# Softmax numerators turned without their scale, and a scale on the attention's output that comes by way of the memory

## The chip, the cores and the metric

One Trainium2 chip, one core. The metric is the device time of one launch in microseconds. The kernel is one hand-scheduled program: each engine (TensorE or PE, VectorE or DVE, ScalarE or ACT, GpSimd or POOL, and SP, which issues DMAs) has its own written list of steps, and semaphores order them.

## The reference

Two layers on x (4 batches of 256 tokens, width 256), each with an attention over a context (4 x 256 x 128) and a feed-forward part. What the change touches is the second layer's attention, 16 query heads in 8 pairs, each pair with one key/value head:

```python
q = (text_hidden @ Wq).reshape(B, T_text, N_HEADS, HEAD_DIM).transpose(0, 2, 1, 3)
k = (vision_tokens @ Wk)...; v = (vision_tokens @ Wv)...      # 8 heads, repeated for 16
scores = jnp.einsum('bhtd,bhsd->bhts', q, k) / scale
scores = jnp.where(mask, scores, -jnp.inf)
attn = jax.nn.softmax(scores, axis=-1)
out = jnp.einsum('bhts,bhsd->bhtd', attn, v)
return out.reshape(B, T_text, N_HEADS * HEAD_DIM) @ Wo
```

Ahead of it stand the first layer (attention without heads, then an 8-bit feed-forward part with ternary weights) and a layer norm, behind it the last feed-forward part (8-bit float weights, three products).

## The kernel before, in words

The second attention runs over n = 0 to 31: batch n // 8, pair of heads n % 8, both heads of the pair at once. For each n, in order:

- `queries(n)` (PE), then `q_hi` (ACT) and `q_lo` (DVE): each operand of a product is split in a high and a low part, and each product is three matmuls.
- `scores(n, h)` (PE) for head h; `masked(n, h)` (DVE) adds the mask, takes the row minimum and writes `sm`, which has two buffers (n % 2), each of four tiles k = 0 to 3 (head and token tile) of 128 tokens x 256 keys.
- `exps(n, h)` (ACT): the exponentials, in place, with their row sums in `ssum`.
- `inverse(n)` (DVE, L1569): the reciprocals `srec` of the four sums. `normalise(n)`: ACT multiplies tiles 0 and 1 of `sm` by them (L998), POOL tiles 2 and 3 (L661).
- The probabilities are turned, so that keys lie on the partitions. For n = 0, 1, 2, 30 and 31 PE does it (`probs4`). For the 27 pairs n = 3 to 29, `turn_blocks(n)` (DVE, L1580) turns 32 x 32 blocks of `sm` into the one buffer `blocks`; `blocks_written(n)` (SP, L441) writes it in four DMAs to `block_room` in the memory, and `blocks_read(n)` (L454) reads it back in two halves c as `tp`, rows now in their right places. `turn_blocks(n+1)` waits until all four writes of pair n have landed. `block_room` and `tp` have two rooms each; a read into `tp` waits until `contexts(n-2)` is done.
- `probs(n, c)` (ACT, L992) makes `pT_hi` from `tp`, `probs_low(n, c)` (POOL, L666) makes `tp_lo`.
- `contexts(n, c)` (PE): the attention's output, transposed, in one PSUM bank. `outputs(n)` (ACT, L1004) makes `oT_hi` from the bank, `outputs_low(n)` (DVE, L1594) makes `oT_lo` = bank - `oT_hi`. `attn_out(n, h)` (PE) multiplies by the fused output weights and sums over the batch's heads in bank 6.

The steps of several pairs are interleaved with each other, with the feed-forward tiles of the first layer's other batches (`gate_half`, `value_half`, `ffn_out`), with the rounding of the last part's weights (`eighths`), and near the end with the last part's products (`gate4`, `up4`, `down`). The order of every engine is a written list of calls at the end of its block, and `PASSING` is the written list of which PSUM bank each product uses, in PE's order. Between `scores(n)` and `contexts(n)` PE works on four or five other pairs.

Of the kernel before, what the change touches and what calls it, by code (L numbers as in the profile page):

```python
# [23 lines left out]
def xattn_ffn_kernel(nc, x, ctxT, mask, wq0T, bq, wk0T, bk, w_norm, wgvT, woutT, wq, wk, wv, wo,  # L24
# [29 lines left out]
    with ExitStack() as ctx:  # L54
# [63 lines left out]
        with ExitStack() as ffn:  # L118
            wgv8 = tile(ffn, "wgv8", [P, KD, 2 * HID], BF16)
            wout8 = tile(ffn, "wout8", [P, KH, D], BF16)  # L120
            wn = tile(ffn, "wn", [P, D])
            gbuf = tile(ffn, "gbuf", [P, 2, TB, D])
# [21 lines left out]
            wscale = tile(ffn, "wscale", [P, 2])  # L144
        with ExitStack() as last:
# [6 lines left out]
        tile(ctx, "ffn_room", [P, 9368])  # L152
# [27 lines left out]
        oT_hi = tile(ctx, "oT_hi", [P, 2, 2 * TOK], F32R)  # L180
        oT_lo = tile(ctx, "oT_lo", [P, 2, 2 * TOK], F32R)
# [7 lines left out]
        block_room = nc.dram_tensor("block_room", [2 * S, 2 * TOK], F32).ap()  # L189

# [3 lines left out]
        def bank16(n):  # L194
# [32 lines left out]
        pT_lo_pool, norm_act = sem("pT_lo_pool"), sem("norm_act")  # L227
# [26 lines left out]
        PASSING = [("project", 0, 4), ("context", 0, 2), ("xn", 0, 3), ("energy", 0, 4), ("project", 1, 5), ("xn", 1, 6),  # L254
                   ("probs", 0, 7), ("energy", 1, 0), ("mean", 0, 4), ("mix", 0, 2), ("project", 2, 7), ("project", 3, 0),
                   ("kv", 0, 2), ("probs", 1, 7), ("energy", 2, 6), ("mix", 1, 7), ("energy", 3, 5), ("kv", 1, 1), ("xn", 2, 0),
                   ("kv", 2, 7), ("kv", 3, 0), ("hidden_in", 0, 4), ("mean", 1, 3), ("probs", 2, 2), ("mix", 2, 4),
                   ("gate", 0, 5), ("gate", 1, 2), ("gate", 2, 7), ("value", 0, 1), ("value", 1, 3), ("value", 2, 5),
                   ("vo", 0, 0), ("probs", 3, 7), ("gate", 3, 3), ("xn", 3, 0), ("value", 3, 2), ("turn", 0, 3), ("vo", 1, 7),
                   ("gate", 4, 6), ("turn", 1, 1), ("vo", 2, 0), ("value", 4, 4), ("turn", 2, 5), ("qk", 0, 6), ("qk", 1, 3),  # L260
                   ("gate", 5, 1), ("vo", 3, 2), ("gate", 6, 4), ("hidden", 0, 1), ("hidden", 1, 0), ("out", 0, 5),
                   ("out", 1, 0), ("turn", 3, 4), ("value", 5, 7), ("vo", 4, 2), ("gate", 7, 5), ("mix", 3, 1), ("turn", 4, 5),
# [7 lines left out]
                   ("gate", 10, 0), ("s", 13, 7), ("q", 7, 1), ("gate", 11, 3), ("rows", 1, 2), ("ctx", 3, 0), ("s", 14, 3),  # L270
                   ("s", 15, 4), ("q", 8, 5), ("q", 9, 2), ("q", 10, 4), ("s", 16, 7), ("s", 17, 1), ("ctx", 4, 7),
                   ("s", 18, 1), ("s", 19, 2), ("value", 9, 1), ("ctx", 5, 5), ("value", 10, 2), ("value", 11, 0), ("s", 20, 3),
# [3 lines left out]
                   ("s", 29, 7), ("out", 4, 0), ("out", 5, 2), ("ctx", 10, 3), ("value", 12, 0), ("rows", 2, 5), ("s", 30, 4),  # L276
# [96 lines left out]
        def as_f32(ap):  # L373
            return ap.bitcast(F32)
# [5 lines left out]
        def _(sp):  # L380
# [51 lines left out]

            def blocks_written(n):
                k = turns_before(n)
                sp.wait_ge(blocks_done, k + 1)
                if k >= 2:
                    sp.wait_ge(blocks_in[0], 16 * (k - 1))
                    sp.wait_ge(blocks_in[1], 16 * (k - 1))
# [2309 lines left out]
```

## Time and profile before

| | |
|---|---|
| median of 3 runs | 319.15 us (318.28 to 320.42) |
| profiled execution | 319.45 us, its span 317.4 us |
| mean granted TensorE clock | 0.993 |
| busy, share of the span | PE 93%, PEld 82%, ACT 81%, DVE 79%, POOL 69% |
| DMA | 44.59 MB in 54609 packets, mean 140 GB/s |

The span runs from the first to the last instruction of the profiled execution; the run's time has 2.05 us beside it. PEld is the loading of weights, beside PE's matmuls. Matmuls are pipelined, so a busy PE need not be at its peak: a 128x256 matmul lasts 283 ns in the rows, and in a dense stretch one begins each 120 ns.

### The profile page before, as it was taken

The page shows a single profiled execution, that of the slowest core. Times are in us where ns is not written, and L with a number is a line of the kernel's source. Part 1 is how long each engine was busy: PE and PEld are TensorE (multiplying, and loading weights), DVE is VectorE, ACT ScalarE, POOL GpSimd, SP SyncE. Part 2 cuts the span into 40 slices and gives each one's busy share as a digit, 9 for nine tenths or more (in the row PEclk, how much of TensorE's full clock was granted, in tenths as well). Part 3 has the DMA queues.
Part 4 walks back from the last instruction along what each step waited for, and adds up shares of the span by engine and source line. Part 5 has one row for each costly group of instructions (what it writes and reads, how often), then busy time and mean ns, then how long its engine had stood idle before and what let it go on. Part 6 is the DMA issues. An engine that isn't in the chain of part 4 may idle for free.

```text
span 317.4 us, 6401 instructions
## 1 busy us (share of the span) xinstructions
PE 294.9 (93%) x1981; PEld 258.8 (82%) x1992; DVE 252.2 (79%) x713; ACT 258.5 (81%) x607; POOL 217.9 (69%) x290
## 2 busy tenths in 40 slices
PE   3676999999999999999989999999999999999994
PEld 2465566889988987899779989889999998989784
DVE  3789698989888789888889788897877595766674
ACT  0869796489999989999997897788899998975350
POOL 3786663566887788797877897878897696772001
PEclk9999799999999999999999999999999999999999
DMA  7994602002046867678637566687665466200201
GB/s 219 380 350 135 176 0 68 1 1 76 5 81 179 245 168 199 165 209 202 180 88 207 150 179 162 165 221 203 147 188 151 116 197 200 69 2 0 68 1 66
DMA packets 54609, 44.59 MB, mean 140 GB/s; under 512 B 11696, under 2 KB 45104, under 8 KB 54576
## 3 DMA queue, kind: packets, MB, share of 16 engines
q1 hardware_dynamic: 54016, 43.93, 49.1%
q8 instruction: 16, 0.26, 0.4%
q10 hardware_dynamic: 560, 0.26, 0.3%
q14 instruction: 17, 0.14, 0.1%
HBM read 27.01 MB, written 15.20 MB: 133 GB/s over the span
## 4 chain that ended last, share of the span: by engine, by line
PE 21%; ACT 15%; POOL 8%; issue 5%; DVE 1%; ACTq 0%; POOLq 0%; DVEq 0%
PE pb L2015 14%; PE pb L2278 4%; ACT sm L980 4%; POOL tp_lo L666 4%; ACT pT_hi L992 3%; PE pb L2312 2%; POOL xn L588 1%; ACT sm L998 1%; ACT L980 1%; POOL sm L661 1%; ACT L1019 1%; ACT fuse L1019 1%; ACT q_hi L975 1%; ACT oT_hi L1004 1%; POOL rstd L582 1%
## 5 line engine op out<-in xcount | busy, mean ns | idle before, releaser
L666 POOL TENSOR_TENSOR tp_lo<-tp,pT_hi 128x512 fp32r<-128x512 f32 x54 | 69.2, 1297 | 20.9 <-ACT pT_hi L992 20.8
L980 ACT ACTIVATE sm<-sm,smin 128x256 f32<-128x256 f32 x128 | 63.6, 503 | 1.1 <-DVE smin L1563 0.7
L1563 DVE CUSTOM_DVE_ANT_0 sm<-pb,mask_all 128x256 f32<-128x256 f32 x128 | 47.5, 419 | 4.0 <-PE pb L2015 3.6
L1580 DVE STREAM_TRANSPOSE blocks<-sm 128x1024 f32<-128x1024 f32 x27 | 33.5, 1240 | 7.0 <-DMA block_room<-blocks 6.1
L2015 PE MATMUL pb<-ctx_hi,q_hi 128*128 128x256 f32 x128 | 37.8, 295 | 0.5 <-DVE q_lo L1550 0.4
L2015 PE MATMUL pb<-xT_hi,m_hi 128*128 128x256 f32 x128 | 37.2, 291 | 0.1
L2015 PE MATMUL pb<-n_hi,oT_hi 128*128 128x256 f32 x128 | 37.1, 290 | 0.1
L2015 PE MATMUL pb<-xT_hi,m_lo 128*128 128x256 f32 x128 | 36.2, 283 | 0.0
L2015 PE MATMUL pb<-xT_lo,m_hi 128*128 128x256 f32 x128 | 36.2, 283 | 0.0
L2015 PE MATMUL pb<-ctx_hi,q_lo 128*128 128x256 f32 x128 | 36.2, 282 | 0.0
L2015 PE MATMUL pb<-ctx_lo,q_hi 128*128 128x256 f32 x128 | 36.1, 282 | 0.0
L2015 PE MATMUL pb<-n_lo,oT_hi 128*128 128x256 f32 x128 | 36.1, 282 | 0.0
L2015 PE MATMUL pb<-n_hi,oT_lo 128*128 128x256 f32 x128 | 36.1, 282 | 0.0
L661 POOL TENSOR_SCALAR sm<-sm,srec 128x256 f32<-128x256 f32 x64 | 30.4, 488 | 8.3 <-DVE srec L1569 8.2
L992 ACT ACTIVATE pT_hi<-tp 128x512 fp32r<-128x512 f32 x54 | 32.2, 623 | 3.4 <-PE pb L2015 3.2
L2015 PE MATMUL pb<-pT_hi,cr_hi 128*128 128x512 f32 x64 | 27.1, 424 | 2.3 <-POOL tp_lo L666 1.6
L998 ACT ACTIVATE sm<-sm,srec 128x256 f32<-128x256 f32 x64 | 28.6, 504 | 0.7 <-DVE srec L1569 0.7
L582 POOL TENSOR_TENSOR rstd<-ve,nhalf 128x2 f32<-128x2 f32 (+1 forms) x16 | 13.3, 834 | 20.1 <-DVE ve L1412 17.4
L1594 DVE TENSOR_TENSOR oT_lo<-pb,oT_hi 128x512 fp32r<-128x512 f32 x32 | 21.7, 681 | 6.0 <-ACT oT_hi L1004 5.9
L2015 PEld LDWEIGHTS pb<-ctx_hi,q_hi 128*128 128x128 f32 x128 | 24.4, 190 | 2.4 <-DVE q_lo L1550 0.9
L2015 PEld LDWEIGHTS pb<-n_hi,oT_hi 128*128 128x128 f32 x128 | 24.4, 191 | 1.4 <-DVE oT_lo L1594 0.5
L975 ACT ACTIVATE q_hi<-pb 128x512 fp32r<-128x512 f32 x32 | 18.8, 588 | 8.0 <-PE pb L2015 7.9
(195 smaller groups left out, 946.4 us busy)
## 6 DMA issues: line engine op xcount, KB each, us to landing
block_room<-blocks SPq DMA_DIRECT2D x108, 128.0 KB, 2.5
tp<-block_room SPq DMA_DIRECT2D x54, 256.0 KB, 3.1
w_raw<-in_w SPq DMA_DIRECT2D x4, 576.0 KB, 4.2
wraw<-in_wgvT SPq DMA_DIRECT2D x4, 512.0 KB, 7.4
wraw<-in_woutT SPq DMA_DIRECT2D x2, 512.0 KB, 10.6
out<-xb SPq DMA_DIRECT2D x4, 256.0 KB, 2.2
xa<-in_x SPq DMA_DIRECT2D x3, 256.0 KB, 4.6
xb<-in_ctxT SPq DMA_DIRECT2D x2, 256.0 KB, 6.1
```

What stands on the lines that cost most here:

```text
L582: g.tensor_tensor(rstd[:, planes, tiles(b)], ve[:, planes, tiles(b)], nhalf[:, planes, tiles(b)], ALU.pow).then_inc(rstd_done, 1)
L661: g.tensor_scalar(sm[:, n % 2, k, :], sm[:, n % 2, k, :], srec[:, n % 2, k:k + 1], 1.0, ALU.mult, ALU.mult).then_inc(norm_done, 1)
L666: g.tensor_tensor(tp_lo[:, z, c, :], tp[:, z, c, :], as_f32(pT_hi[:, c, :]), ALU.subtract).then_inc(pT_lo_pool, 1)
L975: a.activation(q_hi[:], bank(passing_bank("q", n)), ACT.Copy, scale=-SCALE).then_inc(q_hi_done, 1)
L980: a.activation(sm[:, n % 2, k, :], sm[:, n % 2, k, :], ACT.Exp, bias=smin[:, n % 2, k:k + 1], scale=-1.0, accum_out=ssum[:, n % 2, k:k + 1 ...
L992: a.activation(pT_hi[:, c, :], whole, ACT.Copy).then_inc(pT_hi_done, 1)
L998: a.activation(sm[:, n % 2, k, :], sm[:, n % 2, k, :], ACT.Identity, scale=srec[:, n % 2, k:k + 1]).then_inc(norm_act, 1)
L1563: v.tensor_tensor_reduce(out=sm[:, n % 2, k, :], in0=bank(passing_bank("s", 2 * n + h))[:, (k % 2) * S:(k % 2 + 1) * S], in1=mask_all[:, b ...
L1580: v.transpose(blocks[:].rearrange("p g k b -> p k g b"), sm[:, n % 2, :, :].rearrange("p k (g b) -> p k g b", b=32)).then_inc(blocks_done, 1)
L1594: v.tensor_tensor(oT_lo[:, n % 2, :], bank(passing_bank("ctx", n)), as_f32(oT_hi[:, n % 2, :]), ALU.subtract).then_inc(oT_lo_done, 1)
L2015: last = t_.matmul(dst, a_, b_, start=start and k == 0, stop=stop and k == n - 1, skip_group_check=check)
L2278: last = t_.matmul(dst, weight[:, k, i * P:(i + 1) * P], part[:, k, tok], start=n == 0, stop=n == 2 * KD - 1)
```

## The change

For the pairs turned by blocks (n = 3 to 29) the exponentials aren't multiplied by `srec`. They are turned, written, read back and used by `contexts` as they are. The reciprocals take a way of their own: `inverse(n)` writes them 32 times side by side (`sr`, 128 x 4 x 32), a second transpose in `turn_blocks(n)` turns them (`sr_turned`, 128x128), a fifth DMA in `blocks_written(n)` writes four partitions of it (pieces of 32 floats) to `factor_room`, and `factors_read(n)` reads the row of 512 factors back onto all 128 partitions as `rb` (two buffers). It counts on the same semaphore as the second half of `tp`. `outputs_scaled(n)` on VectorE multiplies the bank by `rb` into `o_raw`, from which ScalarE makes `oT_hi` and GpSimd `oT_lo`. ScalarE's `normalise` is gone; for the five other pairs GpSimd scales all four tiles. `down` waits for its own piece of the last weights in place of all. All five engines' lists and `PASSING` are written anew, with the same steps otherwise.

```diff
@@ SP @@
 def blocks_written(n):
     k = turns_before(n)
-    sp.wait_ge(blocks_done, k + 1)
+    sp.wait_ge(blocks_done, 2 * (k + 1))
...
     for i in range(4):
         sp.dma_start(rows[:, :, i * P:(i + 1) * P], blocks[32 * i:32 * (i + 1), :, :, :].rearrange("a g k b -> a g (k b)")).then_inc(blocks_out, 16)
+    sp.dma_start(factor_room[k % 2, :].rearrange("(k i b) -> i k b", k=2 * TB, b=32),
+                 sr_turned[0:P:32, :].rearrange("i (k b) -> i k b", b=32)).then_inc(blocks_out, 16)

+def factors_read(n):
+    k = turns_before(n)
+    if k >= 2:
+        sp.wait_ge(o_scaled, k - 1)
+    sp.wait_ge(blocks_out, 80 * (k + 1))
+    if k >= 1:
+        sp.wait_ge(blocks_in[1], 32 * k)
+    sp.dma_start(rb[:, k % 2, :], factor_room[k % 2:k % 2 + 1, :].broadcast_to([P, 2 * TOK])).then_inc(blocks_in[1], 16)
@@ GpSimd @@
 def normalise(n):
     pool.wait_ge(srec_done, n + 1)
-    for k in (2, 3):
+    for k in range(4):
...
+def outputs_low(n):
+    if n == FIRST_TURNED:
+        pool.wait_ge(oT_lo_done, n)
+    pool.wait_ge(oT_hi_done, n + 1)
+    g.tensor_tensor(oT_lo[:, n % 2, :], o_raw[:, n % 2, :], as_f32(oT_hi[:, n % 2, :]), ALU.subtract).then_inc(oT_lo_done, 1)
@@ ScalarE @@
 def probs(n, c):
     if by_blocks(n):
-        act.wait_ge(blocks_in[c], 16 * (turns_before(n) + 1))
+        act.wait_ge(blocks_in[c], (16, 32)[c] * (turns_before(n) + 1))
...
-def normalise(n):
-    act.wait_ge(srec_done, n + 1)
-    for k in (0, 1):
-        a.activation(sm[:, n % 2, k, :], sm[:, n % 2, k, :], ACT.Identity, scale=srec[:, n % 2, k:k + 1]).then_inc(norm_act, 1)

 def outputs(n):
-    act.wait_ge(oT_ps, n + 1)
+    if by_blocks(n):
+        act.wait_ge(o_scaled, turns_before(n) + 1)
+        whole = o_raw[:, n % 2, :]
+    else:
+        act.wait_ge(oT_ps, n + 1)
+        whole = bank(passing_bank("ctx", n))
     if n >= 2:
         act.wait_ge(attn_ps, n - 1)
-    a.activation(oT_hi[:, n % 2, :], bank(passing_bank("ctx", n)), ACT.Copy).then_inc(oT_hi_done, 1)
+    a.activation(oT_hi[:, n % 2, :], whole, ACT.Copy).then_inc(oT_hi_done, 1)
@@ VectorE @@
 def inverse(n):
     dve.wait_ge(exp_done, 4 * (n + 1))
-    v.reciprocal(srec[:, n % 2, :], ssum[:, n % 2, :]).then_inc(srec_done, 1)
+    if by_blocks(n):
...
+        v.reciprocal(sr[:, n % 2, :, :], ssum[:, n % 2, :].rearrange("p (k a) -> p k a", a=1).broadcast_to([P, 4, 32])).then_inc(srec_done, 1)
+    else:
+        v.reciprocal(srec[:, n % 2, :], ssum[:, n % 2, :]).then_inc(srec_done, 1)

 def turn_blocks(n):
     k = turns_before(n)
-    dve.wait_ge(norm_act, 2 * (n + 1))
-    dve.wait_ge(norm_done, 2 * (n + 1))
+    dve.wait_ge(srec_done, n + 1)
     if k >= 1:
-        dve.wait_ge(blocks_out, 64 * k)
+        dve.wait_ge(blocks_out, 80 * k)
...
     v.transpose(blocks[:].rearrange("p g k b -> p k g b"), sm[:, n % 2, :, :].rearrange("p k (g b) -> p k g b", b=32)).then_inc(blocks_done, 1)
+    v.transpose(sr_turned[:], sr[:, n % 2, :, :].rearrange("p k b -> p (k b)")).then_inc(blocks_done, 1)

+def outputs_scaled(n):
+    dve.wait_ge(oT_ps, n + 1)
+    dve.wait_ge(blocks_in[1], 32 * (turns_before(n) + 1))
+    dve.wait_ge(attn_ps, n - 1)
+    v.tensor_tensor(o_raw[:, n % 2, :], bank(passing_bank("ctx", n)), rb[:, turned_room(n), :], ALU.mult).then_inc(o_scaled, 1)
@@ TensorE @@
 def down(c, n):
...
-    if c == 0 and n == 0:
-        pe.wait_ge(w8_done, B * EIGHTS)
+    if c < KI:
+        pe.wait_ge(w8_done, -(-(2 * KD * INNER + (i + 1) * D) // PIECE))
@@ SP's list, from blocks_written(14) on (one stretch of the new order) @@
 blocks_written(14)
 blocks_read(14)
 blocks_written(15)
+factors_read(14)
 blocks_read(15)
 blocks_written(16)
+factors_read(15)
 blocks_read(16)
 blocks_written(17)
+factors_read(16)
@@ the end of GpSimd's list @@
+outputs_low(28)
 normalise(31)
+outputs_low(29)
+eighths(15)
+eighths_out(15)
 rows4(2)
-eighths(15)
-eighths_out(15)
 rows4(3)
@@ VectorE's list before added3(3); stats4(2) stood ahead of outputs_low(26) @@
+outputs_low(30)
 outputs_low(31)
+stats4(2)
+fuse_low(3)
 added3(3)
 stats4(3)
```

## Rows read from the trace of the kernel before

**Rows 1.** The page, busy times: us, share of the span, instructions of each engine.

```profile
PE 294.9 (93%) x1981; PEld 258.8 (82%) x1992; DVE 252.2 (79%) x713; ACT 258.5 (81%) x607; POOL 217.9 (69%) x290
```

**Rows 2.** Windows of the span: busy us of each engine, clock, DMA share, GB/s.

```profile
0.00:20.00 20.00, 11.44 (x50) 9.27 (x51) 12.29 (x42) 10.08 (x24) 11.91 (x25) 1.00 0.90 303
20.00:40.00 20.00, 15.70 (x80) 10.93 (x80) 16.28 (x51) 16.47 (x31) 14.46 (x21) 0.91 0.62 197
40.00:60.00 20.00, 19.04 (x122) 13.37 (x122) 18.45 (x46) 14.56 (x23) 11.84 (x14) 1.00 0.09 27
60.00:100.00 40.00, 39.38 (x297) 35.54 (x299) 35.08 (x116) 36.34 (x93) 25.59 (x39) 1.00 0.20 49
100.00:160.00 60.00, 58.53 (x418) 52.85 (x422) 50.34 (x148) 58.67 (x140) 49.18 (x62) 1.00 0.72 196
160.00:220.00 60.00, 58.18 (x418) 53.06 (x419) 51.03 (x155) 49.52 (x137) 49.37 (x63) 1.00 0.65 171
220.00:280.00 60.00, 59.84 (x401) 54.45 (x400) 44.83 (x123) 56.54 (x136) 46.37 (x57) 1.00 0.55 150
280.00:300.00 20.00, 19.41 (x131) 17.40 (x131) 13.77 (x24) 10.84 (x19) 7.95 (x12) 1.00 0.04 14
```

**Rows 3.** What PE waited for, 60 to 317.4 us: us in total, times, longest.

```profile
PE pb L2015 <- POOL tp_lo L666: 1.6, 3, 1.1
```

**Rows 4.** Groups of instructions by line: busy us, mean ns, then idle time before.

```profile
L666 POOL TENSOR_TENSOR tp_lo<-tp,pT_hi 128x512 fp32r<-128x512 f32 x54 | 69.2, 1297 | 20.9 <-ACT pT_hi L992 20.8
...
L1580 DVE STREAM_TRANSPOSE blocks<-sm 128x1024 f32<-128x1024 f32 x27 | 33.5, 1240 | 7.0 <-DMA block_room<-blocks 6.1 <-ACT sm L998 0.5
...
L661 POOL TENSOR_SCALAR sm<-sm,srec 128x256 f32<-128x256 f32 x64 | 30.4, 488 | 8.3 <-DVE srec L1569 8.2
L998 ACT ACTIVATE sm<-sm,srec 128x256 f32<-128x256 f32 x64 | 28.6, 504 | 0.7 <-DVE srec L1569 0.7
...
L1594 DVE TENSOR_TENSOR oT_lo<-pb,oT_hi 128x512 fp32r<-128x512 f32 x32 | 21.7, 681 | 6.0 <-ACT oT_hi L1004 5.9
...
L1569 DVE RECIPROCAL srec<-ssum 128x4 f32<-128x4 f32 x32 | 5.4, 170 | 9.4 <-ACT sm L980 9.1
...
L1426 DVE RECIPROCAL erec<-esum 128x2 f32<-128x2 f32 x4 | 0.6, 159 | 0.1
```

**Rows 5.** VectorE's timeline, the first, two adjoining and the last block transpose: start, us.

```profile
93.95 1.25 DVE L1580 STREAM_TRANSPOSE blocks<-sm 128x1024 f32<-128x1024 f32 x1
...
219.41 1.25 DVE L1580 STREAM_TRANSPOSE blocks<-sm 128x1024 f32<-128x1024 f32 x1 [0.85 <-DMA block_room<-blocks]
...
225.09 1.25 DVE L1580 STREAM_TRANSPOSE blocks<-sm 128x1024 f32<-128x1024 f32 x1 [1.14 <-DMA block_room<-blocks]
...
265.32 1.25 DVE L1580 STREAM_TRANSPOSE blocks<-sm 128x1024 f32<-128x1024 f32 x1
```

**Rows 6.** DMA issues: size, median us to landing; then `blocks`' writes, minimum to maximum.

```profile
block_room<-blocks SPq DMA_DIRECT2D x108, 128.0 KB, 2.5
tp<-block_room SPq DMA_DIRECT2D x54, 256.0 KB, 3.1
...
dsc<-in_down_scale SPq DMA_DIRECT2D x1, 128.0 KB, 3.8
...
gsc<-in_gate_scale SPq DMA_DIRECT2D x1, 3.0 KB, 3.6
...
DMA to landing us min/median/max: 2.0/2.5/4.2
```

**Rows 7.** SP's queue, two stretches (219 to 226, 232 to 234 us): start, us.

```profile
219.36 0.82 SPq L454 DMA_DIRECT2D tp<-block_room  x2
220.68 2.38 SPq L441 DMA_DIRECT2D block_room<-blocks  x4
...
232.46 1.84 SPq L441 DMA_DIRECT2D block_room<-blocks  x4
```

**Rows 8.** Waits of the whole span: us in total, times, longest.

```profile
DVE blocks L1580 <- DMA block_room<-blocks: 6.1, 10, 1.1
```

More of the change, by code:

```diff
@@ L1168, in _ @@
+            outputs(5)
+            exps(9, 1)
+            queries(11)
+            probs(7, 0)
+            probs(7, 1)
             exps(10, 0)
-            probs(7, 0)
-            outputs(5)
-            normalise(9)
+            probs(8, 0)
+            outputs(6)
             exps(10, 1)
-            probs(7, 1)
-            queries(11)
-            normalise(10)
             rounded(4)
-            outputs(6)
-            probs(8, 0)
+            probs(8, 1)
             outputs(7)
-            probs(8, 1)
@@ L1752, in _ @@
             outputs_low(1)
-            turn_blocks(3)
+            m_low(7)
             masked(5, 0)
             masked(5, 1)
+            q_low(6)
+            turn_blocks(4)
             second(2)
+            second(3)
+            third_stats(1)
+            outputs_low(2)
+            masked(6, 0)
             inverse(5)
-            q_low(6)
-            second(3)
-            turn_blocks(4)
-            third_stats(1)
-            masked(6, 0)
-            outputs_low(2)
-            masked(6, 1)
@@ L1765, in _ @@
-            q_low(7)
-            turn_blocks(5)
-            eighths(2)
-            gated_half(4, 0)
-            third_low(1)
-            inverse(6)
+            turn_blocks(5)
+            masked(6, 1)
+            eighths(2)
+            outputs_scaled(3)
+            inverse(6)
+            third_low(1)
+            gated_half(4, 0)
+            q_low(7)
+            turn_blocks(6)
             masked(7, 0)
+            q_low(8)
             masked(7, 1)
-            turn_blocks(6)
-            q_low(8)
+            masked(8, 0)
@@ L1775, in _ @@
             inverse(7)
-            outputs_low(3)
-            masked(8, 0)
+            q_low(9)
+            gated_half(4, 1)
+            outputs_scaled(4)
+            turn_blocks(7)
             masked(8, 1)
-            q_low(9)
-            turn_blocks(7)
-            inverse(8)
-            masked(9, 0)
-            outputs_low(4)
-            masked(9, 1)
-            q_low(10)
-            gated_half(4, 1)
-            eighths(3)
+            q_low(10)
+            masked(9, 0)
+            masked(9, 1)
@@ L1788, in _ @@
+            eighths(3)
+            outputs_scaled(5)
+            inverse(8)
+            turn_blocks(8)
             u_max(4)
+            u_scales(4)
+            gated_half(5, 0)
+            masked(10, 0)
             inverse(9)
-            turn_blocks(8)
-            masked(10, 0)
-            gated_half(5, 0)
-            u_scales(4)
+            turn_blocks(9)
             masked(10, 1)
-            outputs_low(5)
-            turn_blocks(9)
-            inverse(10)
+            outputs_scaled(6)
@@ L1798, in _ @@
             gated_half(5, 1)
+            eighths(4)
             q_low(11)
             u_max(5)
-            eighths(4)
-            outputs_low(6)
+            outputs_scaled(7)
+            masked(11, 0)
+            q_low(12)
             u_scales(5)
-            masked(11, 0)
+            inverse(10)
+            turn_blocks(10)
+            outputs_scaled(8)
             masked(11, 1)
-            q_low(12)
-            turn_blocks(10)
+            masked(12, 0)
+            masked(12, 1)
@@ L1808, in _ @@
             inverse(11)
-            outputs_low(7)
-            masked(12, 0)
             q_low(13)
-            masked(12, 1)
-            outputs_low(8)
             turn_blocks(11)
-            inverse(12)
-            added3(0)
-            masked(13, 0)
-            masked(13, 1)
-            eighths(5)
-            q_low(14)
+            masked(13, 0)
+            added3(0)
+            eighths(5)
+            outputs_scaled(9)
+            masked(13, 1)
+            q_low(14)
+            second(4)
@@ L1821, in _ @@
+            inverse(12)
             inverse(13)
             turn_blocks(12)
+            second(5)
             masked(14, 0)
-            outputs_low(9)
-            second(4)
             masked(14, 1)
-            second(5)
             third_stats(2)
+            outputs_scaled(10)
+            turn_blocks(13)
+            q_low(15)
+            eighths(6)
             gated_half(6, 0)
-            q_low(15)
-            turn_blocks(13)
-            outputs_low(10)
-            eighths(6)
@@ L1834, in _ @@
             third_low(2)
+            masked(15, 0)
             inverse(14)
-            masked(15, 0)
+            outputs_scaled(11)
+            gated_half(6, 1)
             masked(15, 1)
-            outputs_low(11)
+            u_max(6)
+            q_low(16)
+            inverse(15)
             turn_blocks(14)
-            gated_half(6, 1)
-            inverse(15)
-            q_low(16)
+            masked(16, 0)
             stats4(0)
             eighths(7)
-            masked(16, 0)
+            outputs_scaled(12)
@@ L1891, in _ @@
             third_stats(3)
-            outputs_low(17)
+            outputs_scaled(17)
             masked(22, 0)
@@ L1932, in _ @@
             eighths(13)
-            outputs_low(22)
+            inverse(26)
             turn_blocks(26)
-            fused(0)
+            outputs_scaled(23)
+            q_low(29)
             masked(28, 0)
@@ L1938, in _ @@
             masked(28, 1)
-            outputs_low(23)
-            q_low(29)
-            inverse(28)
             eighths(14)
@@ L2661, in _ @@
             contexts(31, 1)
+            down(2, 1)
             attn_out(30, 0)
```

971 lines of the change are left out of this document (486 added, 485 removed), and 51 rows, old and new, of the table PASSING.

## The prediction

> **What bounds the kernel now.** I read the busy times first [rows 1]: TensorE 93%, the other four engines' busy shares between 69% and 82%. A busy share is an average, so the windows come next [rows 2]. From 60 to 280 us TensorE is idle for 0.62, 1.47, 1.82 and 0.16 us of its windows (window minus PE busy), and for 0.59 us from 280 to 300: 4.7 us in 240 us. Before 60 us it is idle for 8.6 + 4.3 + 1.0 = 13.8 us, and of the 22.5 us that it idles in all (317.4 less 294.9) the last 4.0 lie behind 300 us, where the last output is scaled, added and stored. In the window from 20 to 40 us the granted clock is 0.91, so part of it ran at the lower level (1.2 of 2.4 GHz) after a stretch with much idle time; no other window to 300 us shows that. The third view is what PE waited for from 60 us on [rows 3]: GpSimd's `tp_lo` 1.6 us in three waits; every other line waited less. So this is a TensorE-bound kernel with two soft spots: the start, and about 5 us of small waits. The change doesn't alter the number or the shape of the matmuls, so beyond these two it can give nothing.
>
> Of the other engines ScalarE is the nearest to a bound: 58.7 of 60 us from 100 to 160, 56.5 of 60 from 220 to 280 [rows 2]. Yet PE waits on it for next to nothing, so relieving it is worth at most what PE idles.
>
> **The change part by part** (27 of the 32 pairs of heads are turned by blocks).
>
> ScalarE loses all its `normalise` work: 64 instructions, 28.6 us busy [rows 4], 0.45 us each. Nothing else is added there; `outputs` reads SBUF for PSUM at the same shape. Per turned pair 0.9 us goes. A pair takes 6.59 us (171.4 us from the first to the last block transpose over 26 steps [rows 5]), so 60 us hold 9.1 pairs and the window of 58.7 us falls to 50.5.
>
> GpSimd loses two scalings of a turned pair, 0.95 us (L661, 30.4 us over 64 [rows 4]), and gains `outputs_low`. Its nearest row is L666, the same subtraction of 128x512 in SBUF: 1.30 us. Net +0.35 us a pair, and 0.95 us more for each of the five unturned pairs: 9.4 + 4.8 = 14 us, hidden as GpSimd goes from 49.4 to 52.6 of 60 us [rows 2].
>
> VectorE swaps `outputs_low` (0.68 us, PSUM and SBUF, L1594) for `outputs_scaled`, a multiplication of the same shape and sources: zero. The reciprocal grows from 4 to 128 columns, and there is a second block transpose, of 128x128. The trace has neither. The big transpose takes 1240 ns for 1024 columns [rows 4]; with a fixed part like the reciprocal's 170 ns that is 1.04 ns a column, so 0.30 us for 128 columns (lower end: an eighth, 0.16). For the reciprocal, 2 columns took 159 ns and 4 took 170. The lower end is no growth, the upper is that slope, 5.5 ns a column, +0.68 us. I take +0.13 us, the pace of the transpose, because four columns can't carry a slope of a few ns. So +0.43 us a pair, 51.0 to 54.9 of 60 us from 160 to 220: hidden.
>
> The latency of a pair changes on both sides. Ahead of the transpose 0.9 us goes. Behind `contexts` the chain was ScalarE 0.6, VectorE 0.7; now it is VectorE 0.7, ScalarE 0.6, GpSimd 1.3: 1.3 us more. The written order gives PE other work between `contexts(n, 1)` and `attn_out(n, 0)`, for turned pairs never less than 36 matmuls, as between `contexts(4, 1)` and `attn_out(4, 0)`. At one matmul in 0.144 us (60 us over 418 [rows 2]) these are 5.2 us against a chain of 2.6 us. I cost it at nothing; without that cover it would be up to 1.3 us a pair. The new wait in `outputs_scaled` is on the landed factors; behind it in VectorE's queue stand `masked` and `q_low`, for which PE waits. But `probs(n, 1)` on ScalarE already waits for the same count before PE can do `contexts`, so it is never late there. It is late, if at all, at `probs(n, 1)`: a broadcast of 128 rows took 3.8 us to land against 3.1 us for a half of `tp` [rows 6], plus 0.4 us of issue, so 1.1 us more; for 11 pairs `factors_read(n)` stands behind `blocks_written(n+1)`, with five issues of 0.46 us ahead: some 3 us. A half of `tp` can be read once `contexts(n-2)` is done, that is two steps (13.2 us) less one contexts (1.4 us) ahead; 3.5 us to land, 1.2 and 2.6 us on ScalarE and GpSimd leave 4.5 us. It holds on average, and not where two contexts come close. GpSimd already waits 20.8 us for `pT_hi` [rows 4], so this cover is thin: I put 0.5 us on it.
>
> SP's queue gets two more issues a pair: the factors' write (0.46 us) and read (0.4 us). It had 1.8 to 2.4 us of issue for the four writes (1.84 us are 0.46 for one) and 0.8 for the reads, in 6.59 us [rows 7], so it has room. But `blocks` is one buffer, and `turn_blocks(n+1)` waits until all of pair n's writes have landed. That loop is the tightest thing in the trace: 219.41 to 225.09 us is 5.68 us [rows 5], VectorE stood still for 1.14 us of it, and in 10 of 27 cases it waited so [rows 8]. With the change it gains 0.25 us (the small transpose, less overlap) and the fifth issue, 0.46 us, whose landing may come sooner than a block's (2.0 us at the least, 2.5 in the median) or later (a small load took 3.6 us [rows 6]). That is +0.0 to +1.6 us, and the loop comes to 5.9 to 7.5 us. I take +0.4 and 6.3, near the blocks' own rows, since it is a write to the same memory in the same queue. PE's own pace is 6.59 less its idle time there (3.4 us over 26), 6.46 us. So it holds the pace by a hair, and costs nothing in sum; uneven steps cost perhaps 0.5 us.
>
> The Trainium skill speaks against this write (DMA: Bandwidth & Descriptors, section Specifications): below 512 bytes a transfer is done as read-modify-write. The pieces here are 128 bytes, and no row of before has a write of that size. By the blocks' rows the loop costs nothing, by the rule it would be rival (b).
>
> The broadcast adds 256 KB to a pair's 1 MB: the DMA share from 100 to 160 us of 0.72 [rows 2] becomes 0.9 at the most. Landings of the writes queued behind it may come later; that is in the loop's upper end.
>
> The two ends and the orders: all five hand-written orders and the banks are laid out anew. The start depends on loads and on the first batch's chain, which the change doesn't touch; `gate_value(0)` is loaded one transfer earlier, two transposes move. I count zero, with 4 us either way as the bounds (a third of the 13.8 idle us). At the end `normalise(31)` takes four scalings on GpSimd, 1.9 us instead of 0.93 beside ScalarE's 0.9, ahead of `outputs_low(29)`, and `stats4(2)` moves in front of `added3(3)`: +0.5 us. Splitting the wait for `w8` lets one `down` go earlier, worth nothing where PE is busy.
>
> Sum: of 4.7 us of idle time after 60 us I give back half, since ScalarE was 98% busy in 100 to 160 and its lateness is behind part of `tp_lo`'s: -2.4. Then +0.5 probs, +0.5 loop, +0.5 end: -0.9. From the profiled 319.45 us (span 317.4, 2 us around it) that is 318.5; the median of the runs is 0.3 lower, so **318.2 us**.
>
> **The rivals.**
> (a) *All waits go.* ScalarE's relief and the new order return the whole 4.7 us and 2 to 4 us of the start: 319.15 - 7 = 312. For it: ScalarE is the fullest engine beside PE and gives up 8 us of 60. Against: PE hardly waited for it.
> (b) *The block buffer becomes the bound.* Once the loop exceeds 6.46 us, each further tenth costs 26 x 0.1 = 2.6 us. With a late landing of the factors, loop 6.8 us: +8.8 less the waits it replaces (3.4), 324.5; at 7.5 us, 343. For it: the loop's 10 waits, the fifth write, the fuller DMA. Against: the buffer ran at 5.5 to 5.7 us, and 6.3 is below the pace.
> (c) *The wide reciprocal is slow.* At the upper slope VectorE gets +0.98 us a pair, 8.9 us per window of 60: 59.9 of 60. With no slack its waits for others' results in the turned stretch can't be absorbed; half of the 12 us or so that it has there: +6, 325. It decides above 0.8 us for 128 columns. The skill has a rule for this (VectorE: DVE Perf Modes, First, the fixed hardware budget): a reciprocal is an iterated divide with a repeat count of 8. With VectorE at 0.96 GHz (Trainium Kernel Development and Optimization, NeuronCore Architecture) that is an estimate of 8.3 ns a column, a microsecond more for 128, and this rival would be the forecast. The 11 ns that two columns more took are below its 17, which speaks rather against it.
> (d) *Nothing moves:* PE is the bound and the waits only change their place, 319. This is within the forecast's own case.
>
> **How the numbers follow.** One per cent, 3.2 us, is about what can be told from no change here. The forecast with (d): 0.50, of which 0.06 falls below 316 and 0.04 above 322.3. (a) 0.24. (b) 0.19, (c) 0.07. So faster 0.30, within 1% 0.40, slower 0.30. The likeliest case's own range is 315 to 322; to hold 8 in 10 I go to 311.5, which takes in (a), and to 326, which takes in (c) and (b) up to a loop of 6.9 us.
>
> **What would show it.** PE idle time from 60 to 300 us below 4.7 us, the busy times of ScalarE near 230 us, GpSimd 232, VectorE 264. `sr` near 0.30 us. Block transposes 6.3 us apart where they wait for the landing, and 26 steps in 168 to 172 us; more than 175 is (b). `pT_hi` of the second half waiting for the factors' broadcast would show in PE's waits for `tp_lo`. The prediction is wrong if the start moves by more than 4 us, if the write of 128-byte pieces lands after 3 us or more, or if the reciprocal takes over 0.8 us.

## The result and the profile after

The changed kernel takes 346.04 us (median of 3 runs, 346.03 to 347.15) against 319.15: the ratio is 1.0831, 95% interval 1.0754 to 1.0908. The forecast was 318.2 and its range ended at 326, so it was wrong by 27 us. The profiled run is 346.04 us with a span of 344.2. Where single executions of an experiment fell into a slower state of the chip, its time below is the median of the others, while some expectations name the median of all.

The page of the kernel after, busy times, to be read against [rows 1]:

```profile
PE 302.6 (88%) x1981; PEld 259.3 (75%) x1992; DVE 276.5 (80%) x740; ACT 238.2 (69%) x543; POOL 232.6 (68%) x273
```

No engine is full. PE's 1981 matmuls are the same ones, in 27 us more of span. The windows of the kernel after, against [rows 2]:

```profile
60.00:100.00 40.00, 37.41 (x272) 32.73 (x273) 35.20 (x107) 30.45 (x77) 27.33 (x41) 1.00 0.25 64
100.00:160.00 60.00, 55.05 (x374) 47.40 (x376) 51.15 (x138) 45.74 (x113) 41.81 (x42) 0.97 0.70 194
160.00:220.00 60.00, 50.37 (x344) 44.38 (x346) 51.85 (x140) 42.09 (x97) 45.41 (x49) 0.97 0.69 177
220.00:280.00 60.00, 56.38 (x382) 50.50 (x381) 49.89 (x130) 42.77 (x110) 46.75 (x48) 1.00 0.66 188
```

PE idles 2.6, 5.0, 9.6 and 3.6 us here, 20.8 in all, where it idled 4.1. It does 1372 matmuls in these 220 us where it did 1534; at 0.144 us each that is 23 us, so some 6 us more are inside its busy time. The granted clock is 0.97 in two windows, those in which PE stood for 5.0 and 9.6 us, so short parts of them ran at the lower of the two levels. That can be part of the 6 us, but it isn't the cause of the loss: o8 below is 17 us slow at a granted clock of 1.00.

VectorE's timeline, the first, a pair in the middle and the last block transpose, against [rows 5]:

```profile
92.66 1.25 DVE L1608 STREAM_TRANSPOSE blocks<-sm 128x1024 f32<-128x1024 f32 x1 [0.61 <-PE pb L2053]
...
129.55 1.25 DVE L1608 STREAM_TRANSPOSE blocks<-sm 128x1024 f32<-128x1024 f32 x1
...
136.61 1.25 DVE L1608 STREAM_TRANSPOSE blocks<-sm 128x1024 f32<-128x1024 f32 x1 [1.55 <-DMA factor_room<-sr_turned]
...
289.85 1.25 DVE L1608 STREAM_TRANSPOSE blocks<-sm 128x1024 f32<-128x1024 f32 x1 [1.57 <-DMA factor_room<-sr_turned]
```

The first stands 1.3 us earlier than before, the last 24.5 us later: 197.2 us over 26 steps, 7.58 us a step for 6.59. These 25.8 us are practically the whole loss. It is made evenly in the turned stretch; the start is unchanged, and from the last transpose to the end it is 54.4 us for 52.1.

The groups by line in the kernel after, against [rows 4]:

```profile
L723 POOL TENSOR_TENSOR oT_lo<-o_raw,oT_hi 128x512 fp32r<-128x512 f32 x27 | 35.5, 1315 | 9.9 <-ACT oT_hi L1060 9.9
L1608 DVE STREAM_TRANSPOSE blocks<-sm 128x1024 f32<-128x1024 f32 x27 | 33.4, 1238 | 8.5 <-DMA factor_room<-sr_turned 7.6 <-PE pb L2053 0.6
...
L1596 DVE RECIPROCAL sr<-ssum 128x128 f32<-128x128 f32 x27 | 25.6, 947 | 1.1 <-ACT sm L1037 0.9
...
L1616 DVE TENSOR_TENSOR o_raw<-pb,rb 128x512 f32<-128x512 f32 x27 | 18.2, 674 | 5.7 <-PE pb L2053 5.1 <-DMA tp<-block_room 0.6
L1060 ACT ACTIVATE oT_hi<-o_raw 128x512 fp32r<-128x512 f32 x27 | 16.9, 624 | 10.0 <-DVE o_raw L1616 10.0
...
L1609 DVE STREAM_TRANSPOSE sr_turned<-sr 128x128 f32<-128x128 f32 x27 | 7.3, 269 | 0.0
```

The reciprocal took 947 ns for the forecast 300. The others cost what was forecast. But new waits stand beside them: ScalarE 10.0 us for `o_raw`, GpSimd 9.9 us for `oT_hi`, and these in a list of waits of the kernel after (60 to 330 us; us in total, times, longest), against [rows 3, 8]:

```profile
POOL tp_lo L717 <- ACT pT_hi L1049: 23.6, 21, 2.3
...
ACT pT_hi L1049 <- DMA rb<-factor_room: 8.6, 6, 3.5
DVE blocks L1608 <- DMA factor_room<-sr_turned: 7.6, 9, 1.6
ACT pT_hi L1049 <- DMA tp<-block_room: 6.4, 4, 2.7
PE pb L2053 <- POOL tp_lo L717: 6.0, 8, 1.7
...
PE pb L2053 <- POOL oT_lo L723: 3.0, 3, 1.7
```

No line of it is 27 us. Every stage of the pair waits a little for the one before, so this list alone doesn't tell which of them is the cause.

### The profile page after: what moved, and what is told of

It reads as the page before. It is cut to its first block, busy times and chain, and to the rows that moved or that the text cites. A ratio compares the mean times of both kernels' runs of the same rounds, so it can differ in the third digit from the quotient of the medians.

```text
span 344.2 us, 6468 instructions
## 1 busy us (share of the span) xinstructions
PE 302.6 (88%) x1981; PEld 259.3 (75%) x1992; DVE 276.5 (80%) x740; ACT 238.2 (69%) x543; POOL 232.6 (68%) x273
## 4 chain that ended last, share of the span: by engine, by line
PE 40%; ACT 16%; DMA 15%; DVE 11%; issue 6%; SPq 5%; POOL 5%; DVEq 0%; ACTq 0%; POOLq 0%
PE pb L2053 24%; DMA factor_room<-sr_turned 6%; PE pb L2315 4%; SPq L450 4%; ACT sm L1037 4%; DMA rb<-factor_room 2%; DVE sr L1596 2%; PE pb L2350 2%; PE pb L2128 2%; DMA w_raw<-in_w 2%; ACT pT_hi L1049 2%; DMA tp<-block_room 2%; DVE q_lo L1574 2%; POOL tp_lo L717 2%; ACT q_hi L1032 1%
## 5 line engine op out<-in xcount | busy, mean ns | idle before, releaser
L1049 ACT ACTIVATE pT_hi<-tp 128x512 fp32r<-128x512 f32 x54 | 33.3, 626 | 29.1 <-PE pb L2053 14.0
L723 POOL TENSOR_TENSOR oT_lo<-o_raw,oT_hi 128x512 fp32r<-128x512 f32 x27 | 35.5, 1315 | 9.9 <-ACT oT_hi L1060 9.9
L2053 PE MATMUL pb<-pT_hi,cr_hi 128*128 128x512 f32 x64 | 27.9, 436 | 9.0 <-POOL tp_lo L717 6.0
L2053 PEld LDWEIGHTS pb<-xT_hi,m_hi 128*128 128x128 f32 x128 | 24.8, 194 | 5.2 <-DVE xT_lo L1563 3.2
L1574 DVE SCALAR_TENSOR_TENSOR q_lo<-pb,q_hi 128x512 fp32r<-128x512 f32 x32 | 21.6, 675 | 8.8 <-ACT q_hi L1032 8.8
```

The source lines that it names most:

```text
L723: g.tensor_tensor(oT_lo[:, n % 2, :], o_raw[:, n % 2, :], as_f32(oT_hi[:, n % 2, :]), ALU.subtract).then_inc(oT_lo_done, 1)
L1049: a.activation(pT_hi[:, c, :], whole, ACT.Copy).then_inc(pT_hi_done, 1)
L1574: v.scalar_tensor_tensor(q_lo[:], bank(passing_bank("q", n)), -SCALE, as_f32(q_hi[:]), ALU.mult, ALU.subtract).then_inc(q_lo_done, 1)
L2053: last = t_.matmul(dst, a_, b_, start=start and k == 0, stop=stop and k == n - 1, skip_group_check=check)
```

## The experiments

The kernel before, run beside them, took 319.1 to 319.6 us. The first four expectations name their theories in words. After them: L, several costs of nearly equal weight that cover one another; O, the changed kernel's own written orders; C, the longer chain from a context to its outputs; N, the removal of the normalising.

**One cost of the changed kernel at a time.** e1: the reciprocal on 4 columns again (`sr` cleared once, 4 of 128 columns written):

```diff
-v.reciprocal(sr[:, n % 2, :, :], ssum[:, n % 2, :]...broadcast_to([P, 4, 32]))
+v.reciprocal(sr[:, n % 2, :, 0], ssum[:, n % 2, :])
```

> The changed kernel (346.04 us) with the reciprocal on 4 columns (one per tile) in place of 128: only one column of each 32 is used after the transpose, so the result is the same. Theory R, the wide reciprocal (947 ns against 170, 27 times, 21 us of VectorE) is the main cause: 325 us or less. Theory L, the landing of the fifth write in the one-buffer loop is the main cause: VectorE's freed time turns into waiting for the landing, 339 to 343 us. Theory O, the new order of the lists is the cause: 340 to 346 us.

345.2 us, ratio 1.0799 (1.0777 to 1.0822). VectorE's busy time fell from 276.5 to 260.6 us, and its wait for the factors' write rose from 7.6 to 14.0 us. Much of the freed time became waiting.

e2: the factors' transpose and write ahead of the blocks':

```diff
+v.transpose(sr_turned[:], ...)
 v.transpose(blocks[:]..., sm...)
-v.transpose(sr_turned[:], ...)
```

> The changed kernel with the factors' transpose and their write put ahead of the blocks' transpose and writes, so that the fifth write's issue and landing lie beside the big transpose. Nothing is left out. The loop from one block transpose to the next, now some 7.0 us where it waits, would be 6.0 to 6.3. Theory L: 26 steps of 0.7 us and more come back, 325 to 330 us. Theory R: 342 to 346 us, and the waits for the landing vanish from VectorE's rows. Theory W, that the second half of the probabilities waits for the factors' read: no change beyond 2 us.

346.59 us, 1.0838 (1.0766 to 1.0911). It gives nothing back.

e3: no traffic of the factors (the outputs are multiplied by ones, so the division is left out):

```diff
-sp.dma_start(factor_room[...], sr_turned[0:P:32, :]...)
-factors_read(n)                       # all 27
+v.memset(rb[:], 1.0)                  # once
```

> The changed kernel without the factors' write and read; the outputs are multiplied by ones, so the attention's outputs of the 27 pairs are not divided by their sums. The wide reciprocal, both transposes, the multiplication and all orders stay. It removes at once the fifth issue, its landing, the read's issue, its traffic and the wait for it at the second half of the probabilities. Theory L or W: 322 to 328 us. Theory R: 338 to 344 us. Theory O: 340 or more.

339.02 us, 1.0624 (1.0595 to 1.0653): 7 us come back, 20 stay.

e4: a semaphore of its own for the read, so that `probs(n, 1)` doesn't wait for it:

```diff
-sp.dma_start(rb[...], ...).then_inc(blocks_in[1], 16)
+sp.dma_start(rb[...], ...).then_inc(factors_in, 16)
```

> The changed kernel with a semaphore of its own for the factors' read, so that the second half of the probabilities waits for its own half alone, and only the multiplication waits for the factors. Theory W (ScalarE waited 8.6 us for that read, the engine behind it 6 us more): 335 to 339 us. Theories R and L: 343 to 346 us.

345.74 us, 1.0825 (1.0773 to 1.0878). It gives nothing back, though ScalarE's 8.6 us of waits for `rb` are gone.

**Costs together, and the orders.** o1: both costs out of the changed kernel (e3 with the edit of e1; no division):

> Third experiment plus the narrow reciprocal: the changed kernel's five written orders, with the factors neither written nor read (the outputs are multiplied by ones, so the division by the sums is left out for the turned pairs) and the reciprocal again on 4 columns. What is left of the change is the ordinary multiplication by ones on DVE, the small transpose, the subtraction moved to GpSimd and the new orders. Theory L (several loops of nearly equal length, each hiding the others, so that one alone taken out gives nothing back): with the two costs of the loop both out the time falls to 318 to 326 us. Theory O (the new written orders are slow by themselves, whatever the costs): it stays at 333 to 339 us, near the 339.0 us with the factors' traffic alone left out.

336.99 us, 1.0547 (1.0491 to 1.0602). Theory L falls as it stood: 17.6 us stay with both costs gone.

e5: the three repairs (e1, e2, e4) in one kernel, nothing left out:

> The changed kernel with all three repairs at once, nothing left out of the computation: the reciprocal on 4 columns, the small transpose and the factors' write ahead of the blocks', and a semaphore of its own for the factors' read. Theory L: the step between block transposes falls from 7.58 to 6.7 to 7.1 us and the time to 326 to 337 us. Theory O: 341 to 346 us, as with each repair alone.

340.99 us, 1.0684 (1.0622 to 1.0745): 5 us come back.

For theory O the changed kernel's work was put into the written orders of before. My first placing put each scaling on VectorE early in that list (one place of it; the subtraction goes to GpSimd):

```diff
 eighths(8)
+outputs_scaled(14)
 turn_blocks(16)
...
-outputs_low(14)
```

> All the work of the changed kernel, the wide reciprocal and the factors' traffic included, but issued in the written orders of the kernel before: the scalings stand on DVE as soon as their contexts can be there, the subtractions on GpSimd before the next probabilities but one, the factors' read right behind the blocks' read. Theory O: 319 to 328 us. Theory L: 340 to 352 us, since every cost is still there.

> The orders of the kernel before (as in the run above) with the reciprocal on 4 columns and a semaphore of its own for the factors' read; the whole computation is there. Theory O: 316 to 322 us, the reciprocal's 25 us on DVE now worth little. Theory L: 326 to 338 us, as much as the same repairs give in the new orders. Were it under 319 us it would beat both kernels.

466.21 us (o2) and 447.36 us (o3, a single execution; its three others took 457 to 824 us, so it has no ratio). They test nothing of theory O. The waits of o2 (60 to 450 us) say what happened:

```profile
DVE o_raw L1616 <- PE pb L2053: 148.5, 26, 10.9
ACT sm L1037 <- DVE smin L1587: 70.7, 21, 9.4
```

VectorE stood 148.5 us at the head of its queue for contexts, with `masked` and `q_low` behind it, for which ScalarE and PE waited. Scalings a few steps too early (that of pair 14 stands eight steps ahead of its place in o5) cost 109 us between o2 and o5, the dependent steps on ScalarE and GpSimd placed anew with them. So the next three took each place from the trace of before: `outputs_scaled(n)` ahead of the first step that began after `contexts(n)` had ended, ScalarE's rounding and GpSimd's subtraction 0.8 and 1.4 us on.

> The whole work of the changed kernel, every cost of it included, issued in the written orders of the kernel before, each new step put at the place in its engine's list at which the trace of the kernel before shows its operands ready: the scaling at the end of the context's last matmul, ScalarE's rounding 0.8 us later, GpSimd's subtraction 0.6 us after that (the runs with the orders of before above put the scaling too early, and DVE stood 148 us waiting for contexts). Theory O (the changed kernel's own written orders are slow): 319 to 330 us. Theory L (the costs in the loop are what is slow, in any order): 340 to 352 us.

> The same orders, with the reciprocal on 4 columns and a semaphore of its own for the factors' read; the whole computation is there. Theory O: 316 to 326 us. Theory L: 328 to 340 us. A third theory, C (the longer chain from a context to its outputs' rounding, over DVE, ScalarE and GpSimd, is what holds it, in any order and with the costs away): within 2 us of 337.

> The same orders, with the reciprocal on 4 columns and no factors' traffic (the outputs are multiplied by ones, so the division by the sums is left out for the turned pairs). Left of the change: ScalarE's normalising gone, the multiplication on DVE, the subtraction on GpSimd. Theory O: 312 to 320 us. Theory C: 330 to 338 us, as the 337.0 us with the same work in the changed kernel's orders. Theory L: 312 to 326 us.

o5 356.89 us (1.1174), o6 352.13 us (1.1017), o8 335.94 us (1.0523, 1.0474 to 1.0573). Theory O falls: without the two costs it is 336 us in these orders and 337 in the new ones. With them the new orders are 11 us better than the old ones as I filled them (346.0 against 356.9).

**The removed part alone.** d1: the turned pairs' `normalise` left out on both engines of the kernel before (no division), nothing added:

```diff
-normalise(n)                          # ScalarE and GpSimd, n = 3 to 29
```

> The kernel before with the removed part alone: the turned pairs' exponentials are not multiplied by their sums' reciprocals, on ScalarE or on GpSimd, and nothing takes the place of it (the division is left out); contexts, rounding and the subtraction on DVE as before. This prices what the change takes away. Theory C (the longer chain from context to outputs is what costs 17 us in both runs without the factors' traffic): 312 to 319 us, so that the chain's steps make the whole difference to 336. Theory N (it is the removal itself that does harm, by moving work together or taking the normalising's slack out of the queues): 328 to 337 us.

316.57 us, 0.9907 (0.9882 to 0.9932). The removal brings 3.0 us; theory N falls. The windows of one stretch, d1 and then o8:

```profile
60.00:300.00 240.00, 236.76 (x1670) 215.13 (x1669) 194.24 (x563) 193.17 (x468) 153.44 (x176) 1.00 0.52 140
```

```profile
60.00:300.00 240.00, 223.13 (x1552) 197.59 (x1560) 195.93 (x572) 184.67 (x447) 185.99 (x204) 1.00 0.53 137
```

VectorE does about the same in both. In o8 PE has 13.6 us less and 118 matmuls fewer.

**The way from the context to the outputs.** d2: o8 with the subtraction on VectorE again (no division):

```diff
-g.tensor_tensor(oT_lo, o_raw, oT_hi, ALU.subtract)     # GpSimd
+v.tensor_tensor(oT_lo, o_raw, oT_hi, ALU.subtract)     # VectorE, behind ScalarE's rounding
```

> The run o8 (orders of before, narrow reciprocal, no factors' traffic, outputs multiplied by ones) with one change: the subtraction of the rounded outputs stands on DVE again (0.68 us from o_raw), where it stood before, in place of GpSimd's 1.30 us. Theory C in the form that it is GpSimd's queue (the subtraction waits there for ScalarE, and the next probabilities' subtraction, 1.3 us twice, stands behind it): 318 to 325 us. Theory C in the form that DVE's scaling ahead of ScalarE's rounding makes the chain too long: 332 to 338 us.

337.59 us, 1.0538 (1.05 to 1.0576). So it isn't GpSimd's queue alone. d4: the scaling out of the chain but not out of the queue. ScalarE and `outputs_low` read PSUM as before; VectorE multiplies as many elements, waiting for the same context, into a tile that nothing reads (no division):

```diff
-act.wait_ge(o_scaled, ...); whole = o_raw[:, n % 2, :]
+act.wait_ge(oT_ps, n + 1); whole = bank(passing_bank("ctx", n))
-v.tensor_tensor(o_raw[...], bank(...), rb[...], ALU.mult)
+v.tensor_tensor(rb[:, 1, :], rb[:, 0, :], rb[:, 0, :], ALU.mult)
```

> The same work on every engine as in d2 (338.2 us), but the scaling is out of the chain: ScalarE rounds the context straight from PSUM as before, DVE subtracts from PSUM as before, and between them DVE makes a multiplication of the same 128x512 elements, which still waits for the context, into a tile that nothing reads (the division is left out). If the length of the chain context, DVE, ScalarE is what costs (DVE's place for the scaling must be late enough for the context and early enough for ScalarE): 318 to 324 us. If it is DVE's load and its wait for the context, whoever waits for it: 332 to 340 us.

323.61 us, 1.0147 (1.0109 to 1.0185). Taking the scaling out of the chain gives back 14.0 us. The edit brings two things with it that weren't tested apart: ScalarE's rounding and VectorE's subtraction stand in their places of the kernel before again (some 30 places in their lists), and the context's bank is freed by the subtraction, not by the scaling. The other 7.0 us over d1 are VectorE's load with its wait, and the smaller parts of the change that d4 keeps. In the profiled runs only 5.1 us of the difference lie between the first and the last block transpose; 2.3 us lie ahead of the first, where no scaling has run yet. What PE waited for (60 to 330 us), first in d4, then in d2:

```profile
PE pb L2016 <- DVE q_lo L1505: 1.7, 4, 0.5
```

```profile
PE pb L2019 <- DVE oT_lo L1571: 7.8, 7, 1.9
...
PE pb L2019 <- DVE q_lo L1509: 3.3, 4, 1.9
PE pb L2019 <- POOL tp_lo L679: 3.0, 3, 1.9
```

and in o8, where GpSimd subtracts:

```profile
PE pb L2020 <- POOL tp_lo L679: 7.7, 15, 1.6
...
PE pb L2020 <- POOL oT_lo L685: 4.0, 4, 2.1
```

With the subtraction on VectorE, PE waits for `oT_lo` itself. With it on GpSimd, it waits for the probabilities' subtraction, which now shares that queue. The length between is in the timelines: from the end of the last matmul of a pair's contexts to the end of its `oT_lo`, mean of the 27 turned pairs, it took 4.4 us in the kernel before, 4.8 in d4, 6.4 in d2 and 6.9 in the kernel after. In o8 it stayed at 4.4, and there PE waits more for the probabilities in the same queue. d2 and d4 aren't equal in VectorE's load either: d2's subtraction took 953 ns and d4's 678, d4's multiplication 823 ns and d2's 681, so VectorE has 5.4 us more in d2. By the price of VectorE's load below that is 1 or 2 of the 14.0 us.

Where the 953 ns come from is in the trace. The subtractions of d2 (both sources in SBUF), then those of d4 (one source in PSUM), minimum, median and maximum in ns:

```profile
L1571 DVE TENSOR_TENSOR oT_lo<-o_raw,oT_hi x27: 650/695/1812, 114.3 to 301.9; 128x512 fp32r<-128x512 f32 x27
```

```profile
L1568 DVE TENSOR_TENSOR oT_lo<-pb,oT_hi x32: 650/683/694, 89.1 to 292.2; 128x512 fp32r<-128x512 f32 x32
```

Of d2's 27, 16 took 650 to 720 ns. The other 11 began while an instruction of GpSimd had 0.29 to 1.26 us left, and each ended 0.54 to 0.55 us after that one. None of d4's 32 did so, though GpSimd worked beside most of them. So an instruction of VectorE with both sources in SBUF waits here for most of GpSimd's running ones (two of d2's 16 began beside an `rstd` and an `xn` and didn't wait), and one with a source in PSUM doesn't.

e6: the same move in the changed kernel with its three repairs, the whole computation there:

> The whole computation of the changed kernel in its own orders with the three repairs of e5 (341.0 us), and the subtraction of the rounded outputs on DVE, behind ScalarE's rounding, in place of GpSimd. DVE goes from 262 to 280 us busy, GpSimd from 232 to 197. Theory C as GpSimd's queue: 324 to 332 us. Theory C as the scaling's place in the chain: 340 to 348 us.

349.37 us, 1.0953 (1.0902 to 1.1004): 8 us worse than e5. Here 21 of the 27 subtractions were held up by GpSimd in that way, and they took 1102 ns in the mean. The subtraction fits neither engine.

**One added cost at a time in the kernel before.** b1: a second reciprocal, 128 columns wide, that nothing reads:

```diff
+v.reciprocal(wide[:], ssum[:, n % 2, :]...broadcast_to([P, 4, 32]))
 v.reciprocal(srec[:, n % 2, :], ssum[:, n % 2, :])
```

> The kernel before with one part of the change alone: for each turned pair DVE makes one more reciprocal, 128 columns wide as in the changed kernel, into a tile that nothing reads. It adds 27 times 0.95 us to DVE, 25.6 us in all, from 252 to 278 us busy. If DVE has room for it (as e1 said of the changed kernel): 319 to 323 us. If DVE's load is itself a loop near the bound, as theory L holds: 325 to 335 us.

324.27 us, 1.0148 (1.0075 to 1.0221): 5 us for 25.4 us of VectorE. That is between its two cases.

The factors' traffic, write and read (b3), and then the write alone (b2):

```diff
 for i in range(4): sp.dma_start(block_room..., blocks...)
+sp.dma_start(factor_room[k % 2, :]..., blocks[0:P:32, 0, :, :]).then_inc(blocks_out, 16)
 for c in range(SC): sp.dma_start(tp..., block_room...)
+sp.dma_start(rb[...], factor_room[...].broadcast_to(...)).then_inc(blocks_in[1], 16)   # b3 only
```

> The kernel before with the factors' traffic alone: a fifth write of 4 partitions in 128-byte pieces behind the four of the blocks, counted with them, and a read of 2 KB into all 128 partitions behind the blocks' read, counted with its second half, on which the second rounding of the probabilities waits; nothing reads what it brings. By e3 against the changed kernel the traffic is worth 7 us: 323 to 329 us. If the traffic costs only in a kernel whose other queues are already late: 319 to 322 us.

> The kernel before with the fifth write alone (4 partitions, 128-byte pieces, counted with the four of the blocks), and no read of the factors. With write and read it took 337.6 us. If the write, which holds the block buffer until it has landed, is the traffic's cost: 332 to 338 us. If it is the read, in SyncE's queue ahead of the next writes and in ScalarE's wait for the probabilities' second half: 319 to 324 us.

With the read it is 335.56 us, 1.0537 (1.0466 to 1.0609), without it 320.26 us, 1.0028 (1.0 to 1.0055). So the write costs 0.6 us and the read about 15. SP's queue in b3:

```profile
183.54 0.82 SPq L461 DMA_DIRECT2D tp<-block_room  x2
184.41 0.43 SPq L464 DMA_DIRECT2D rb<-factor_room  x1
184.95 2.08 SPq L444 DMA_DIRECT2D block_room<-blocks  x4
187.07 0.98 SPq L445 DMA_DIRECT2D factor_room<-blocks  x1
190.38 0.82 SPq L461 DMA_DIRECT2D tp<-block_room  x2
```

VectorE's block transposes began at 183.62 and 190.45; the second waited for the write of 187.07, which by the chain of work took 3.26 us from there to its landing, with the read's 256 KB ahead of it. The waits of b3, VectorE and SP:

```profile
DVE blocks L1590 <- DMA factor_room<-blocks: 21.8, 14, 3.2
```

```profile
SPq L460 <- DMA factor_room<-blocks: 27.0, 13, 2.5
...
SPq L441 <- DMA rb<-factor_room: 20.3, 8, 3.5
...
SPq L461 <- DMA rb<-factor_room: 5.6, 3, 2.9
```

SP now stands 25.9 us for landings of `rb`, at the next pair's writes and at its own reads, and everything behind it in the queue goes later. In the chain of work that ended last, from 95 to 285 us, SP's issues and the landings of its DMAs have 78% and PE's products 5%; in the kernel before these products are the largest part of that chain, with 23%. This is the price of b3's place for the read, right behind the blocks' read; in the kernel after it often stands elsewhere. In the traces the steps between block transposes that ended in a wait for the landing have a median of 6.0 us before (10 steps), 6.55 in b2 (12), 6.93 in b3 (14) and 7.45 in the kernel after (9). PE's pace was 6.46.

## Why the prediction was wrong

The costs as they stack up, each from the run named: 319.6 us before; -3.0 for the removal (d1); +7.0 for VectorE's scaling and small transpose as load (d4); +14.0 for the scaling's place in the chain (d2, with what d4's edit brought along); -1.7 with the subtraction on GpSimd (o8); +21.0 for traffic and wide reciprocal (o5, where b3 and b1 alone gave 16.0 and 5.1); -10.9 for the new orders: 346.0. The sum closes by construction. What speaks for it is that traffic and reciprocal, measured apart in the kernel before, give 21.1 us where they took 21.0 together; b3's interval is 14.9 to 19.5 us, so a match this close is partly luck.

1. *"So beyond these two it can give nothing"; -2.4 for the waits.* Right: d1 gained 3.0.
2. *The outputs' chain, "I cost it at nothing".* This step failed, by 12 to 14 us (d4 against o8 and d2). I added up durations (2.6 us) against a cover of 5.2 us of matmuls, and took the chain before as 1.3 us. It took 4.4 on average, for each step stands in a queue behind others. One more engine adds one more queue: 6.9 us after, more than that cover. The cover was miscounted, too: pair 28 has 30 matmuls in it and not 36, and 12 of pair 4's 36 are `attn_out(3)`, which itself waits for the chain of the pair before. "Without that cover it would be up to 1.3 us a pair" counted one operation and no queue. GpSimd's 20.8 us of waits for `pT_hi` [rows 4] could have warned me that a handover costs more than its operation.
3. *The factors' read, 0.5 us.* This failed, by some 15 us in the kernel before. I priced its lateness at `probs(n, 1)`, the one wait that names it, and e4 shows that this wait was worth nothing in the changed kernel. By the trace of b3 it costs mainly in SP's queue, where the next pair's writes stand behind it and its landing; ScalarE's 11.0 us of waits for `rb` there were not taken apart from it. The prediction had that as "in the loop's upper end" and gave it no term. In the changed kernel write and read together are worth 7.0 (e3).
4. *The fifth write, loop 6.3 us, 0.5 us.* Right in size: 6.55 us and 0.6 us (b2, at most 1.8 by its interval). In the chain of the kernel after its landings took 2.6 to 4.4 us, so my sign of 3 us or more did show, without that price. The Trainium skill's rule of a read-modify-write below 512 bytes (DMA: Bandwidth & Descriptors, Specifications) is neither shown nor refuted by it.
5. *The reciprocal, +0.13 us.* It was +0.78, and as an added load it cost about 5 us (b1). I chose the lower branch on a step of 11 ns between 2 and 4 columns; that step's slope, 5.5 ns, was the right reading, the measured one is 947 less 170 over 124 columns, 6.3 ns. Rival (c) priced this at 325, and b1 took 324.3. It had a chance of 0.07. The Trainium skill's repeat count (VectorE: DVE Perf Modes, First, the fixed hardware budget), an estimate of 8.3 ns a column, was nearer to the measured 6.3 than the 1.0 that I took, and I argued it away.
6. *Rival (b), the block buffer.* Right in direction: 7.45 us in the median of the waiting steps, 343 us at 7.5. But the cause it named, a late landing of the write, is b2's 0.6 us. By b3 against b2 the buffer is slow through what the read does to the queue, and removing the traffic (e3) leaves 20 of 27 us, so it isn't the only bound. That its 343 us lie near 346 is luck.
7. *The orders at zero.* The start was; as a whole they saved 11 us against the old ones as I filled them (o5), and the end cost 2.3 us for 0.5.

The common fault: each cost was weighed by itself against the slack of a pair, 6.59 us of pace with PE at 98%. PE's queue is written in a fixed order, and in it one late context makes the next steps late too. Open is how the 14.0 us divide between the longer wait for `oT_lo`, the delay of the steps queued behind the scaling, the written places and the bank that is freed by another step; d2 and d4 differ in all four.

No version of the change beat the kernel before; the best with the division in it was e5, 341.0 us.

## What to carry to other kernels

Where in-order queues are nearly full, cost a moved step by the handovers it adds, not by its duration: measure the time from producer to final consumer in the trace before, queueing included, and add a queue's share for each new engine in it. A DMA issue is paid by what stands behind it in its queue, and by every wait that its landing enters, not by the wait that names it. And where a trace is to be taken as a planner, a step that waits for another engine goes where the trace shows its operand ready: too early cost over 100 us here. That is a first placing and not the best one; o5, placed so, was 11 us behind the orders of the changed kernel.

## What the runs showed of the hardware

- A fp32 reciprocal on VectorE costs about 6.3 ns a column: 170 ns for 4, 947 ns for 128.
- An instruction of VectorE with both sources in SBUF mostly waits for the one that GpSimd is working on: of d2's 27 subtractions of 128x512 from `o_raw`, 16 took 650 to 720 ns and the 11 others up to 1812, each ending 0.54 to 0.55 us after GpSimd's (mean 953). With a source in PSUM, all 32 of d4's took 650 to 694. Nine of d4's 27 multiplications, from SBUF alone, waited in the same way (mean 823 ns).
- A write of 4 partitions in 128-byte pieces took 0.53 us to issue, for a block's 0.45, and cost 0.6 us in 27 pairs (b2). A read of one 2 KB row into 128 partitions took 3.6 us to land, for 2.9 of half of `tp`, as many bytes.
- 25 us of added VectorE work cost 5 us where it was 79% busy (b1), and d4's 29 us about as much: a busy share well below one is no free room where the work stands in a fixed order.
